# SyncE waits for ScalarE's sign, and no longer for the transpose, before it loads the lower half of a tile of adj

## The reference

```
h = relu(layernorm(x))
# layer 1: hyperbolic graph convolution
xt = logmap0(proj(mobius_add(proj(mobius_matvec(weight, h)), hyp_bias)))     # [4096, 128]
support = adj @ xt                                                          # reads all of adj
x = x + proj(expmap0(relu(logmap0(proj(expmap0(support))))))
# layer 2: attention over the edges of adj
h = relu(layernorm(x))
left, right = (context @ W_common.T) @ w_left + b_left, (context @ W_common.T) @ w_right + b_right
logits = leaky_relu(left[:, None] + right[None, :], 0.2), -inf where adj <= 0
x = x + relu(softmax(logits) @ h)
```

## Time and profile before

| | |
|---|---|
| median of 3 runs | 581.68 us |
| the profiled execution | 582.62 us |
| its span, first to last instruction | 580.8 us |
| mean granted TensorE clock | 0.95 |
| PE, PEld busy | 491.2 us, 314.8 us |
| DVE busy | 456.6 us |
| ACT busy | 320.0 us |
| POOL busy | 268.4 us |
| HBM read, written | 80.02 MB, 4.21 MB |

### The profile page before, as it was taken

The page is one execution under the profiler, slowest core; times in us unless marked ns, Lnnn a source line. Parts: engine busy times, 40 slices in busy tenths (PEclk is TensorE's granted clock), DMA queues, the critical chain, the costliest instruction groups (busy, mean ns, idle before and its releaser), DMA issues.

```text
span 580.8 us, 8551 instructions
## 1 busy us (share of the span) xinstructions
PE 491.2 (85%) x2695; PEld 314.8 (54%) x2695; DVE 456.6 (79%) x916; ACT 320.0 (55%) x490; POOL 268.4 (46%) x325
## 2 busy tenths in 40 slices
PE   0730999999799979996888558799999999999995
PEld 0630444343344334332323436678888888888884
DVE  3797898787888788773668999986969696968773
ACT  1965887685577657664466653433444445453521
POOL 4850017989879897944234998400202111110200
PEclk9985899999799999999899688989999999999998
DMA  7999799999999999999994010101010101111010
GB/s 163 207 222 205 151 250 291 295 298 285 265 254 292 286 293 258 300 286 179 241 246 94 20 36 1 37 19 38 19 38 20 37 19 37 24 32 37 1 37 18
DMA packets 157189, 84.72 MB, mean 146 GB/s; under 512 B 7344, under 2 KB 155056, under 8 KB 157152
## 3 DMA queue, kind: packets, MB, share of 16 engines
q1 hardware_dynamic: 88768, 47.20, 36.9%
q10 hardware_dynamic: 65968, 32.65, 25.1%
q0 software_dynamic: 2416, 4.41, 3.0%
HBM read 80.02 MB, written 4.21 MB: 145 GB/s over the span
## 4 chain that ended last, share of the span: by engine, by line
PE 54%; DVE 17%; DMA 14%; issue 5%; ACT 4%; POOL 3%; ACTq 2%; POOLq 0%; DVEq 0%
PE ps L716 33%; PE ps L690 20%; DMA room<-in_adj_dram 13%; DVE room L976 4%; DVE room L1183 2%; ACTq L739 2%; ACT mask L849 2%; DVE room L1134 1%; DMA mask<-in_x_dram 1%; DVE room L1150 1%; DVE stats L1094 1%; DVE room L1157 1%; DVE mask L986 1%; POOL mask L439 1%; POOL mask L433 1%
## 5 line engine op out<-in xcount | busy, mean ns | idle before, releaser
L690 PE MATMUL ps<-room 128*128 128x512 f32 x512 | 237.0, 614 | 39.4 <-DVE room L1065 19.7
L716 PE MATMUL ps<-room 128*128 128x258 f16 x2048 | 234.2, 278 | 20.9 <-POOL room L611 14.1
L716 PEld LDWEIGHTS ps<-room 128*128 128x128 fp8e4 x2048 | 201.6, 99 | 53.4 <-issue 14.9
L976 DVE STREAM_TRANSPOSE room<-room 128x512 f32<-128x512 f32 x256 | 169.5, 692 | 58.5 <-DMA room<-in_adj_dram 36.6
L849 ACT ACTIVATE mask<-room,constants 128x1024 int8<-128x1024 f32 x128 | 144.7, 1144 | 87.5 <-DVE room L976 83.0
L690 PEld LDWEIGHTS ps<-room 128*128 128x128 f32 x512 | 95.3, 195 | 175.6 <-issue 98.3
L625 POOL TENSOR_TENSOR h_room<-h_room 128x512 f32<-128x512 f32 x7 | 8.9, 1276 | 148.1 <-DVE post L1224 148.1
L1150 DVE SCALAR_TENSOR_TENSOR room<-mask,constants,room 128x512 int32<-128x512 int32 x64 | 62.1, 971 | 7.9 <-ACT room L898 7.6
L898 ACT ACTIVATE room<-relu_u,r_col 128x512 int8<-128x512 f32 x64 | 42.0, 713 | 41.7 <-PE ps L716 41.7
L898 ACT ACTIVATE room<-room,r_col 128x512 int8<-128x512 f32 x62 | 40.9, 712 | 35.6 <-PE ps L716 35.6
L474 POOL TENSOR_TENSOR mask<-mask,h_room 128x2048 f32<-128x2048 f32 x8 | 36.3, 4538 | 46.8 <-DVE room L1065 46.5
(11 more groups left out here) (158 smaller groups left out, 347.6 us busy)
## 6 DMA issues: line engine op xcount, KB each, us to landing
room<-in_adj_dram SPq DMA_DIRECT2D x136, 256.0 KB, 8.4
room<-in_adj_dram ACTq DMA_DIRECT2D x120, 256.0 KB, 9.9
mask<-in_L_gnn_context_dram SPq DMA_DIRECT2D x16, 256.0 KB, 11.6
xk<-in_x_dram POOLq DMA_DIRECT2D x32, 64.0 KB, 6.5
out_dram<-xk POOLq DMA_DIRECT2D x32, 64.0 KB, 5.9
h_room<-out_dram SPq DMA_DIRECT2D x32, 64.0 KB, 2.3
out_dram<-h_room SPq DMA_DIRECT2D x28, 64.0 KB, 1.7
mask<-in_x_dram ACTq DMA_DIRECT2D x8, 128.0 KB, 6.8
```

What stands on the lines that cost most here:

```text
L690: pe.matmul(acc[parity], xt[:, k, :], turned[:, k % TSLOTS, :], start=(k == 0), stop=(k == NK - 1)).then_inc(block_multiplied, 1)
L716: mm = pe.matmul(ps[:, 2 * t + w, 0:GW], part[slot(c, g)][:, kk, t * P:(t + 1) * P], G[w][:, k, :], start=(k == 0), stop=(k == NK - 1))
L976: v.transpose(turned[:, k % TSLOTS, :].rearrange("p (l b i) -> p b l i", l=L, b=NQ), loaded[:, g % XSLOTS, :, l * Q:(l + 1) * Q].rearrange ...
```

## The change

In `load`, SyncE's wait before the two pieces of a lower half names another semaphore. Before, it waited until the four blocks that the slot held were transposed by DVE; now it waits until ACT has written the signs of the same four blocks, the second of the two signs of that tile. The number that it waits for is the same count of blocks, divided by HB. The first four tiles still have no such wait. Nothing else is changed.

```diff
                 for g in range(NC):
                     first_tiles = c == 0 and g < XSLOTS
                     if not first_tiles:
-                        sp.wait_ge(block_turned, c * NK + L * (g - XSLOTS + 1))
+                        sp.wait_ge(half_signed, (c * NK + L * (g - XSLOTS + 1)) // HB)
                     for b in (0, 2, 1, 3) if first_tiles else LOW:
                         sp.dma_start(loaded[b * Q:(b + 1) * Q, g % XSLOTS], adj_n[c, g, b]).then_inc(
                             adj_in[g % XSLOTS], 16)
```

## The result

| | before | changed |
|---|---|---|
| median, 6 runs each | 582.54 us (581.56 to 585.6) | 600.73 us (596.21 to 602.38) |
| ratio, with its 95% interval | | 1.0268 (1.0229 to 1.0308) |
| the profiled execution | 582.62 us | 599.67 us |
| its span | 580.8 us | 597.9 us |

The changed kernel is slower by 2.7%, and its time lies outside the range of the prediction, 576 to 592. (In all that follows medians and ranges are of all runs, and ratios leave disturbed executions out, so that a ratio can differ from the quotient of two medians.)

The account below looks back on a forecast made before the run. The prediction took most of the first layer to wait for bytes of adj, not for the moment of request. Its terms summed to 0 + 0 + 0, so the median stays 581.7 us, with a range of 576 to 592.

Parts of the forecast that it names:

- The moves: 60 SyncE waits name another semaphore, nothing else moves; SP's requests lag ACT's by 1.2 us at least, 4.0 at worst.
- The 1.7 us of the steady part: In the first layer's steady tiles, SP would ask 1.68 us behind ACT, read from one tile's transpose and sign.
- 0.9 us at 291 GB/s: Possible gain per refill of the queues, a tile whole up to about half a piece earlier; some 3 us in all.
- The start: Fifth tile's lower half issued 13.6 us later, hidden by nearly idle DMA engines: cost 0, at most 1.2 us.
- Cost 0, if the engines can run at full rate from what is queued: Steady part and behind DVE's pause: the later lower halves cost nothing; up to 70 us if all cover is gone.
- The cover: What hides the lag: 5.0 us of queueing in the steady part; behind the pause, ACT's half tile, 2.4 us.
- the engines do the same bytes, the upper half first and the lower half second: Claim for first-layer adj loads that moving the tile's halves one after the other costs 0.
- rival B: Fast rate needs both queues deep; fast stretches between 84 and 262 us slow down, 588 to 601 us; chance 0.14.
- Rival A: SP's queue runs dry behind refills and at the worst late sign: 6.3 us slower, 588.0 us; chance 0.22.
- Rival C: ACT's 4.0 us idling behind its DMA issues goes: 577.7 us, or 573 with better slow-stretch rates; chance 0.26.
- SP's landing: Sign of the forecast: SP's median time from issue to landing of a lower piece, 9.0 us, shortens by about 1.7.
- the piece would only queue less long: Steady part: about 5.0 of 9.0 us to landing is queueing, so a lag of 1.7 us shortens queueing only.

Follow-up runs that it names:

- e3: The kernel before, with the new wait for the sign at the fifth tile alone: 585.55 us, ratio 1.0008.
- e9: The kernel before with half pieces, SP rows 0 to 7, ACT rows 8 to 15, both writing the same 32 partitions at about the same time: 616.61 and 632.15 us.
- e5: The kernel before, with all four pieces of every tile issued by SP behind the transpose and none by ACT: 631.36 us, one run, beside 587.13.
- e1: The changed kernel, with ACT also waiting for its own sign, so both halves are asked for at the same moment: 587.7 us, ratio 1.0059.
- e8: The kernel before with each DMA of 262 KB split in two of 131 KB: 581.93 us, ratio 0.9854, 4 runs.
- e13: The kernel before, half pieces dealt by rows, both queues reading the same columns in order, ACT writing two partition groups further on: 589.51 us, one run.
- e15: The kernel before, half pieces dealt by rows, SP taking partition groups 0, 1, 2, 3 and ACT 2, 3, 0, 1: 587.56 us, ratio 1.009.
- e7: The changed kernel with each piece of 262 KB split in two DMAs of 131 KB: 596.69 us, ratio 1.0156 against the kernel before.
- e14: The kernel before with each DMA split in two of 131 KB, the same kernel as e8 with more runs: 582.45 us, ratio 0.9999, 12 runs.

## Why the prediction was wrong

**The moves** were right: no instruction in another place, a lag of 1.2 us at least (1.17 and 1.21 measured), ACT not issuing behind its own sign, and the second layer unchanged. The 1.7 us of the steady part, read from one tile, were too much; the median is the bare sign. One size beside the sum was also wrong: 0.9 us at 291 GB/s is a whole piece of 262 KB and not half a piece.

**The start** was right: cost 0 (e3).

**The step that failed** is "Cost 0, if the engines can run at full rate from what is queued". It has two parts. That something is always queued was right: the DMA share stayed at 1.20. "At full rate" was left as a condition, though the trace of before held the two rates: 223 GB/s for a single queue at 18 to 34 us and 288 to 292 for two. The cover was worked out at that slow rate (0.52 / 0.223 = 2.4 us), as if time bought at 223 GB/s cost nothing beside 291. The sentence before it had "the engines do the same bytes, the upper half first and the lower half second", and took it as free. It is the very thing that costs, because the upper half alone and the lower half alone each move at the slow rate. The measured price in place of the 0 is 16.6 us between the first sign and the last transpose, and 15.6 of them follow from the rates: 46.5 us more in which one queue has over 70% of the bytes, at 226 GB/s.

**The Trainium skill** was weighed there. "DMA: Bandwidth & Descriptors", section "Rules for kernel authors", says that spreading DMAs over the issuing engines gives no bandwidth. Two queues that write the same partitions agree with it: e9 moves 223 to 227 GB/s, e5 with one queue 221 to 227. Two queues that write different halves do not: all pieces from one queue (e5) 631.36 us, from two 587.13. I took the rule as contradicted and gave the contradiction only to rival B.

**Rival A** (the queue runs dry at refills, 588.0) is wrong: none of the stretches read between 84 and 313 us has a DMA share under 1.19, and behind the pause it is 260 GB/s in place of 246.

**Rival B** (588 to 601) named the places and, at its upper end, the time, but that agreement is luck: its 19.4 us were for all three stretches at 239 GB/s. Its signature, stretches between 84 and 262 us at 225 to 260 GB/s, came for one of three (252), nearly for another (264) and not for the third (276). What the three stretches moved before takes some 9.5 us longer at these rates; the rest of the loss lies outside them. And its cause, depth, is wrong: e1 asks for everything later than the changed kernel and loses 0.6%. What spoke against it, the slow rate from 276 to 301 us with full queues, speaks against depth only.

**Rival C** had ACT's 4.0 us go, and they went, for nothing. Its other half, a gain from a better balance, went the other way.

SP's landing was to become 1.7 us shorter. In the stretch from 84 to 145 us its median went from 9.0 to 10.3 us. The pieces of a tile count on one semaphore, so this number mixes the pieces of both queues. Worked out from the bytes that SP's queue moved, the median from a piece's issue to its last byte was 8.3 us before and 8.5 in the changed kernel. So the lag was not taken off the time in the queue, as "the piece would only queue less long" had it: the pieces came later by the lag and queued as long as before.

**What stays open.** Whether the slow rate belongs to one group of 32 partitions or to one half of 64. Why queues that are asked at different moments take turns, and what brings them back into step (the changed kernel finds back for stretches at a time, as from 245 us) was not found either; the trace has packets but not what chooses between them. Nor was the scatter of the kernel before explained, 576.86 to 599.07 us in its 23 runs of the last comparison. No kernel here is surely faster than the one before.

## What to carry to other kernels

Two queues that each fill their own partitions, here one the lower 64 and one the upper 64, are worth their rate only while both are served at once: let them ask for the two halves at the same moment, and if one of them must be late, let the other be late with it. "The engines always have something queued" is no proof that a later request is free; look for two levels of GB/s at an unchanged DMA share, and ask which of them the new order will run at.

## What the runs showed of the hardware

- The DMA engines moved 221 to 231 GB/s while one queue had them (e5, and the one-sided time before) and 223 to 227 with two evenly served queues that went through the same groups of 32 partitions (e9). They moved 263 to 292 with two queues that wrote mostly one below and one above partition 64 (before, e8, e13, e15). The DMA share was 1.19 to 1.23 in all of these stretches but one of e5 (1.14).
- Two queues with a backlog each are not always served evenly: 317 to 92, then 51 to 366 packets in a microsecond. One-sided time was 24 to 41 us where both ask at the same moment, and 46, 78.5, 106 and 122 us at distances of 0.67, 1.17, 1.93 and 2.95 us.
- DMAs of half the size were served more evenly where both queues ask at the same moment (2.0 and 7.0 us one-sided), and not where one asks later (67 us, e7). They cost their issuing engine more: ACT's waits behind issues rose from 4.0 to 21.2 us (16.7 in e14).
